# Scores of two groups in one visit of TensorE, one bank for both FFNs' sums, projections moved in a macaron block on one Trainium2 core

## The reference

```python
x = x + 0.5 * ffn(layernorm(x), w_gate_up, w_proj)
x = x + attention(layernorm(x), Wq, Wk, Wv, Wo)
x = x + 0.5 * ffn(layernorm(x), w_gate_up, w_proj)

def ffn(x, w_gate_up, w_proj):             # hidden width 2048
    gate, up = split(x @ ternary(w_gate_up).T)   # ternary: per 64 weights round(w / mean|w|) * mean|w|, bf16
    return rms_norm(silu(gate) * up) @ ternary(w_proj).T

def attention(x, Wq, Wk, Wv, Wo):          # 32 heads of 16, blocks of 128 tokens
    # each token attends to itself and the 128 tokens before it: its own block of keys and the one before
    return softmax(mask(q k^T / 4)) @ v @ Wo.T
```

## Time and profile before

| | before |
|---|---|
| median of 3 runs | 2028.27 us |
| the profiled execution | 2030.56 us, span 2028.7 us |
| TensorE busy | 1919.7 us, 95% |
| VectorE, ScalarE, GpSimd busy | 1541.2, 1493.1, 510.9 us |
| mean granted TensorE clock | 0.98 |
| share of the transfers' queue | 75.9% |

### The profile page before, as it was taken

The page is one execution under the profiler, slowest core; times in us unless marked ns, Lnnn a source line. Parts: engine busy times, 40 slices in busy tenths (PEclk is TensorE's granted clock), DMA queues, the critical chain, the costliest instruction groups (busy, mean ns, idle before and its releaser), DMA issues. The chain is left out here.

```text
span 2028.7 us, 37471 instructions
## 1 busy us (share of the span) xinstructions
PE 1919.7 (95%) x12447; PEld 898.9 (44%) x12688; DVE 1541.2 (76%) x4079; ACT 1493.1 (74%) x2871; POOL 510.9 (25%) x559
## 2 busy tenths in 40 slices
PE   6678899999999999999999999999999999999887
PEld 3353344444444444444444444444444444444332
DVE  8966788777876888777777888777786788777673
ACT  6837777777776777777776777777776777768672
POOL 2012222232223222322222223222223232221100
PEclk8889999999999999999999999999999999999898
DMA  7336888788887878777896788878886788768772
GB/s 233 121 71 112 147 153 147 132 141 159 149 156 126 156 145 153 136 145 150 154 159 125 138 155 153 149 131 154 159 155 120 141 153 165 144 120 154 131 136 52
DMA packets 1031648, 287.81 MB, mean 142 GB/s; under 512 B 1016096, under 2 KB 1017120, under 8 KB 1030944
## 3 DMA queue, kind: packets, MB, share of 16 engines
q1 hardware_dynamic: 1031456, 285.41, 75.9%
HBM read 25.17 MB, written 8.39 MB: 17 GB/s over the span
## 5 line engine op out<-in xcount | busy, mean ns | idle before, releaser
L731 ACT ACTIVATE masked<-masked,exp_bias,exp_scale 128x256 f32<-128x256 f32 (+1 forms) x1024 | 503.8, 562 | 8.6
L1095 PE MATMUL ps_yy<-wp_t,ht 128*128 128x512 bf16 x1978 | 481.0, 383 | 14.4 <-DMA ht<-hh 11.7
L1049 PE MATMUL ps_gu<-wgu_t,xt_A 128*128 128x512 bf16 x1940 | 473.8, 382 | 11.2 <-DVE hid L859 2.5
L1049 PE MATMUL ps_gu<-wgu_t,xt_C 128*128 128x512 bf16 x1958 | 472.6, 379 | 5.3 <-DMA xt_C<-xh 0.5
L605 ACT ACTIVATE hh<-hid 128x512 f16<-128x512 f32 x256 | 161.0, 629 | 276.3 <-DVE hid L865 271.0
L876 DVE CUSTOM_DVE_ANT_0 masked<-ps_s,mask 128x256 f32<-128x256 f32 (+1 forms) x1024 | 337.4, 385 | 0.7 <-PE ps_s L1085 0.6
L865 DVE SCALAR_TENSOR_TENSOR hid<-ps_gu,h_scale_u,hid 128x512 f32<-128x512 f32 x252 | 188.9, 750 | 185.0 <-PE ps_gu L1049 184.7
L1095 PEld LDWEIGHTS ps_yy<-wp_t,ht 128*128 128x128 f16 x2016 | 197.9, 99 | 254.5 <-DMA ht<-hh 13.5
L1049 PEld LDWEIGHTS ps_gu<-wgu_t,xt_A 128*128 128x128 f16 x2048 | 198.6, 98 | 243.3 <-issue 6.3
L1049 PEld LDWEIGHTS ps_gu<-wgu_t,xt_C 128*128 128x128 f16 x2048 | 193.4, 98 | 222.5 <-issue 2.4
L850 DVE TENSOR_TENSOR prob<-masked,prob 128x1024 f16<-128x1024 f32 (+1 forms) x256 | 278.9, 1089 | 2.4 <-ACT prob L743 2.4
(11 more groups left out here) (148 smaller groups left out, 1892.8 us busy)
## 6 DMA issues: line engine op xcount, KB each, us to landing
stream<-in_L_attn_x_dram SPq DMA_DIRECT2D x32, 256.0 KB, 3.3
pt<-prob SPq DMA_TRANSPOSE x512, 3.2
out_dram<-stream SPq DMA_DIRECT2D x32, 256.0 KB, 2.4
prob<-in_L_ffn_w_gate_up_dram SPq DMA_DIRECT2D x4, 1024.0 KB, 5.6
ht<-hh SPq DMA_TRANSPOSE x256, 3.3
stream<-in_L_ffn_w_gate_up_dram SPq DMA_DIRECT2D x3, 1024.0 KB, 5.6
stream<-in_L_ffn_w_proj_dram SPq DMA_DIRECT2D x2, 1024.0 KB, 4.9
prob<-in_L_ffn_w_proj_dram SPq DMA_DIRECT2D x2, 1024.0 KB, 4.8
```

The lines of the kernel that those rows point to most:

```text
L731: t = act.activation(p, p, ACT.Exp, bias=exp_bias[:, 4 * g + h:4 * g + h + 1], scale=exp_scale[:, 0:1])
L1049: t = pe.matmul(bank[:, :], xt[s][:, part, k, :], wgu_t[:, k, at:at + CH], start=(k == 0 and part == 0), stop=(k == KD - 1 and part == 1))
L1095: t = pe.matmul(ps_y[s][:, :], ht[:, n % HRING, i, :], wp_t[:, 4 * c + i % 4, :], start=(c == 0 and i == 0), stop=(c == NC - 1 and i == 2 ...
```

## The change

- The scores of an even and the odd group after it are issued together in the even step, right behind the gate matmuls; the odd group's go to `ps_x` (the bank that was C's sum) and `ps_m`. VectorE takes the maxima of both in the even step.
- A and C share the bank `ps_y`; the first `down` of a unit sequence waits until the sum before was added.
- PV goes between down and up. The projections are at the steps 8, 10, 12 and 22, all even, and use the bank `ps_u` in steps without a unit, `ps_m` otherwise, where they now wait for the maxima (`bank_free`).
- ScalarE makes the normalised tokens' high part (xh) behind the exps, and the high part of the probabilities ahead of the hidden quarter's. VectorE's low part of the probabilities stands behind the hidden product, at the end of its own step.
- K's transpose is issued in two parts, the first for the pairs of heads 0 to 3. The transposes of the probabilities stand one step earlier in SyncE's program, ahead of ht.

```diff
-    LN_B, XHAT_B, SPLIT_B = 5, 6, 7
-    Q_AT, K_AT, V_AT = 8, 9, 11
+    LN_B, XHAT_B, SPLIT_B = 6, 6, 7
+    Q_AT, K_AT, V_AT = 8, 10, 12
-    PROB = SCORES + 1
-    NORM = PV + 1
-    SPLIT_O, WO_AT = NORM + 7, 23
+    NORM = PV
+    SPLIT_O, WO_AT = NORM + 7, 22
-        ps_y = {"A": ps_yy[:, 0:CH], "C": ps_yy[:, CH:2 * CH]}
+        ps_y, ps_x = ps_yy[:, 0:CH], ps_yy[:, CH:2 * CH]
+        ps_sc = ((ps_s[:, 0:CH], ps_s[:, CH:2 * CH]), (ps_x, ps_m))
...
+        def projected(step):
+            return ps_m if ffn_at(step)[0] else ps_u
...
-                    transpose(kt[:, :, b % BPS, :], k4[:, :, :, :].rearrange("p a b c -> p (a b c)"), t_k)
+                    for part, pairs in enumerate((slice(0, 4), slice(4, HEADS // 2))):
+                        transpose(kt[:, pairs, b % BPS, :],
+                                  k4[:, 2 * pairs.start:2 * pairs.stop, :, :].rearrange("p a b c -> p (a b c)"),
+                                  t_k[part])
...
@@ VectorE, step_of
                 b, g = group_at(step, SCORES)
-                if b is not None:
-                    masked_max(b, g)
+                if b is not None and g % 2 == 0:
+                    masked_max(b, g)
+                    masked_max(b, g + 1)
...
+                b, g = group_at(step, SCORES)
+                if b is not None:
+                    prob_lo(b, g)
...
@@ TensorE, step_of
+            def bank_free(step):
+                if projected(step) is ps_m:
+                    need(pe, d_mx, 2 * groups_by(step + 1, SCORES))
+                else:
+                    s, b, c = ffn_before(step)
+                    if s:
+                        pe.wait_ge(d_h[s], 4 * b + c + 1 + (NC if s == "A" else 0))
...
+                b, g = group_at(step, SCORES)
+                if b is not None and g % 2 == 0:
+                    if step == SCORES:
+                        pe.wait_ge(a_lo, 8)
+                    need(pe, d_mx, 2 * (8 * b + g))
+                    projections_taken(step - 2)
+                    if g == 0:
+                        pe.wait_ge(t_q, 16 * (b + 1))
+                        pe.wait_ge(t_k[0], 16 * (b + 1))
+                    if g == 2:
+                        pe.wait_ge(t_k[1], 16 * (b + 1))
+                    scores(b, g, ps_sc[0])
+                    scores(b, g + 1, ps_sc[1])
```

More of the change, by code:

```diff
@@ L298, in macaron @@
         assert len(AT_STEP) == len(GATES) == 2 * NB * NC - NC
+        assert all(QUARTERS[n][1:3] == QUARTERS[n - n % NC][1:3] for n in range(len(QUARTERS)))
         def gate_at(step):
@@ L453, in _ @@
                 load_x(b)
-            for step in range(FIRST_STEP, STEPS + 1):
+            for step in range(FIRST_STEP, STEPS + 2):
                 b = block_at(step, Q_AT + 1)
@@ L694, in step_of @@
                         act.wait_ge(g_fill, 3)
[L695 to L700, removed]
+                    copy(v[:, b % BPS, :, 0:DK], head_view(projected(step - 1)[:, :]), p_v, b + 1, a_v, 2.0 ** -V_LOG2)
                 if step == LAST_SPLIT:
@@ L733, in step_of @@
                     t.then_inc(a_exp, 1)
-                s, bf, c = ffn_at(step)
-                if s:
-                    hidden_hi(s, bf, c, place(step), 4 * bf + c + 1 + (NC if s == "A" else 0))
+                for s, offset in SPLITS:
+                    b = block_at(step, offset)
+                    if b is not None and in_steps(s, b) and not (s == "B" and b == 0):
+                        split_free(act, step, s)
+                        copy(xh[:, 0, :], xhat[:, :], g_xh[s], b + 1, a_xh[s])
+                b = block_at(step, SPLIT_O)
+                if b is not None:
+                    output_hi(b)
                 b, g = group_at(step, SCORES)
@@ new lines, in step_of @@
+                if step == LAST_WO:
+                    add_output(LAST, ps_m)
+                    norm_stats("C", LAST, d_x2, NB)
+                s, bf, c, n = gate_at(step)
+                if s:
+                    gated(s, bf, c, n)
+                b = block_at(step, LN_B)
+                if b is not None and b > 0:
+                    norm_stats("B", b, d_x1, b + 1)
+                b = block_at(step, LN_C)
+                if b is not None and b < LAST:
+                    norm_stats("C", b, d_x2, b + 1)
@@ L947, in step_of @@
+                b = block_at(step, LN_A)
+                if b is not None and in_steps("A", b):
+                    norm_stats("A", b, x_in[b % 2], 16 * (b // 2 + 1))
                 b, g = group_at(step, NORM)
@@ L993, in step_of @@
                         attention_weight(n)
-                b = block_at(step, WO_AT + 1)
-                if b is not None and b < LAST:
-                    add_output(b)
+                b = complete("A", step, 2)
+                if b is not None:
+                    add_ffn("A", b, d_x1)
+                b = complete("C", step, 2)
+                if b is not None:
+                    add_ffn("C", b, d_x3)
                 s, bf, c = ffn_at(step)
@@ L1069, in attention_weight, with project, scores @@
                 t.then_inc(a_tr, 1)
-            def project(m, tokens, done):
+            def project(m, tokens, done, bank):
                 for k in range(KD):
                     for n, (part, w) in enumerate(((0, wat_hi), (0, wat_lo), (1, wat_hi))):
-                        t = pe.matmul(ps_m[:, :], tokens[:, part, k, :], w[m][:, k, :], start=(k == 0 and n == 0),
+                        t = pe.matmul(bank[:, :], tokens[:, part, k, :], w[m][:, k, :], start=(k == 0 and n == 0),
                                       stop=(k == KD - 1 and n == 2))
                 t.then_inc(done, 1)
-            def scores(b, g):
+            def scores(b, g, banks):
                 at_block = b % BPS
@@ L1083, in scores @@
                         rows = slice(64 * o, 64 * o + 3 * DK)
-                        at = o * CH + pair * 2 * P
-                        t = pe.matmul(ps_s[:, at + P * first_half(b):at + 2 * P],
+                        t = pe.matmul(banks[o][:, pair * 2 * P + P * first_half(b):(pair + 1) * 2 * P],
                                       qt[rows, b % QRING, 2 * g + pair, :],
@@ L1175, in output_projection, with projections_taken @@
                 need(pe, d_x2, b)
-                project(O, ot, p_wo)
+                project(O, ot, p_wo, bank)
+            def projections_taken(step):
+                for offset, done in ((Q_AT, d_q), (K_AT, d_k), (V_AT, d_v), (WO_AT, d_x2)):
+                    b = block_at(step, offset)
+                    if b is not None:
+                        pe.wait_ge(done, b + 1)
             def step_of(step):
                 if step == LAST_WO:
-                    output_projection(LAST)
+                    need(pe, d_mx, 2 * 8 * NB)
+                    output_projection(LAST, ps_m)
                 s, b, c, n = gate_at(step)
```

168 lines of the change are left out of this document (72 added, 96 removed).

## The result

After: 2031.91 us, median of 9 runs (2029.52 to 2037.31). Before, on the same chip: 2027.07 us, median of 9 runs (2025.95 to 2029.26). The ratio over all these executions is 1.0028 (it is not that of the two medians), 95% interval 1.0016 to 1.0039: 0.3% slower, where 2010 us had been forecast. The profiled execution of the changed kernel took 2029.5 us and is among its quickest; the one of before is among its slower ones, so their spans stand 1.1 us apart the other way. The traces tell where the time is, the medians how much.

What follows compares the result with a forecast made beforehand. TensorE was taken to bound the 1657 us middle, latency the 220 us around it. Profiled 2030.6 - 22.6 (pairs) + 4.2 (projection's wait) = 2012.2; the median lies 2.3 below the profiled run, so 2010 us, range 2003 to 2015.

Steps and rivals of the forecast that it cites:

- What bounds the kernel: TensorE bounds the 1657 us middle, where nothing in its step waits; latency bounds 220 us around it.
- Scores in pairs: TensorE goes into the scores half as often in the middle, saving 0.20 us a pair: 113 pairs, -22.6 us.
- Rival A: At the paired scores each group pays the drain: eight matmuls 0.66 us, a pair saves 0.09, time 2022; chance 0.10.
- Wait 1: In even steps the projection waits for VectorE's eight maxima; 0.2 us charged in 21 of 28 blocks, +4.2 us.
- Rival B: VectorE's eighth maximum comes late in even steps and stalls TensorE's projection: slower, put at 2042 us; chance 0.11.
- Normalised tokens' high part behind the exps: ScalarE's copy comes some 3 us later; POOL waits for it, its result is used a step later: hidden.
- All stay hidden, by my count: Reordered transfers on the one queue all land before TensorE wants them; smallest slack 0.3 us, for K's first quarter.
- Rival D: A new block's scores wait for K's first quarter: 0.5 us in 28 blocks, 14 us, time 2024; chance 0.05.
- The ends: Start and end of the kernel, with Q's bank wait of 4.1 us each to be had: set to 0, bounds -8 and +12.
- Rival C: In steps without units a pair pays one group of maxima openly, 11 us in all: 2018 to 2022; chance 0.14.

Runs made afterwards that it cites:

- e1: The changed kernel with ScalarE's high-part copies of A's, B's and C's normalised tokens back ahead of tanh and exps; 2033.69 us, ratio 1.0025 to the kernel before.
- e9: The changed kernel with the first part of K's transpose one place earlier in SyncE's program, ahead of ht; 2039.71 us, ratio 1.0059 to the kernel before.
- e13: The changed kernel with only C's high-part copy of the normalised tokens back ahead of the exps; 2014.23 us, ratio 0.9927 to the kernel before.
- e6: The changed kernel with A's and C's high-part copies ahead of the exps, B's still behind them; 2011.07 us, ratio 0.9908 to the kernel before.
- e12: e6 without pairs: each group's scores and maxima in its own step, all in the scores' bank; 2068.55 us, ratio 1.0196 to the kernel before.
- e2: The changed kernel with K's transpose in one piece again; 2118.67 us, ratio 1.0447 to the kernel before.
- e3: The changed kernel without pairs where one of a pair's two steps has no FFN unit; 2053.4 us, ratio 1.0122 to the kernel before.
- e10: e6 with the down projection as TensorE's last work of a step at both ends; 2011.73 us, ratio 0.9925 to the kernel before.
- e11: e6 with the down projection as TensorE's last work of a step at the end alone; 2010.83 us, ratio 0.9914 to the kernel before.

## Why the prediction was wrong

*What bounds the kernel:* right. The middle is TensorE's pitch, and every wait put there shows in the time: the changed kernel, e1 and e9 have 10.8, 17.6 and 17.9 us of waits there, e13 has 1.9, and their middles are 9.8, 18.0 and 18.6 us longer than e13's.

*Scores in pairs, 0.20 each:* right. Eight matmuls take 0.54 (0.55 forecast), with 128 keys 0.33; four pairs make a block of 57.60 us instead of 58.45, so 0.21 a pair (e6, e13, and e12 the other way). Rival A, 0.66, is out: the fixed part is paid once for two groups behind each other. The Trainium skill (TensorEngine Tiling (Array Packing), Key Properties) says that a change of the tiling mode drains TensorE and a change of tile alone does not. The trace agrees with it as far as the 0.54 us go.

*Wait 1, +4.2:* not needed. The changed kernel has no such wait between the landmarks. The chain is as tight as counted, though: one copy of 0.6 us ahead of it (B's, in e1) makes 19 waits of 0.9. Rival B's place was right, and it does not fire in this kernel.

*The step that failed* is the treatment of the moved copy: "Normalised tokens' high part behind the exps: ... the copy was waited for by POOL, whose result is used a step later. Hidden." POOL's result is used by the multiplications a step later, but its first user is a transpose in SyncE's program, and that one stands ahead of the transposes of the probabilities, ht and K. I followed the copy's data and not the queue behind its reader. With it falls "All stay hidden, by my count": K's first quarter was given 0.3 us of slack from the time its data is ready, as if the queue were free then; it is issued 3.0 us later (996.82 to 999.86). A second error hid a part of this one. The landing was put at up to 4.3 us, the time of the whole transpose, and the first quarter takes at most 2.64. Counted from the odd step's start (994.71), the prediction had K's quarter landed by 7.0 and wanted at 7.3; it was issued at 5.15 and wanted at 7.47 (1002.50 less the wait of 0.32). With the whole transpose's landing time every block would have waited some 2 us, as e2 did.

Rival D named this wait and its size came out (0.5 us in 28 blocks, 14 us, 2024; measured 15.0 us in 24 waits over the run), by luck, since no row gave its 0.5, and it had 0.05 of the chance: I weighed only how long the landing would take. What D's sum lacked is the ends: between the changed kernel and e13 the start differs by 3.3 us (1.4 of it ahead of any copy of C) and the end by 4.9 besides the 9.8 of the middle, 18.0 together in the profiles; the medians 2031.91 and 2014.23 say 17.7, the ratios 1.0028 and 0.9927 some 20.

*The ends, 0:* right for all the rest of the change taken together, by e13, whose start and end are those of before within 0.3 us, in one execution of each. The 4.1 us that were "to be had" at each end were misread in part: the 12 matmuls of Q that take 4.29 us instead of 2.60 stand in a stretch with a granted clock of 0.62 (222.2 to 226.6 us of the kernel before), so 1.7 of the 4.1 are the clock's and not the bank's. Rival C is not borne out as far as it was tried (e3, e12).

With C's copy undone the time falls into the forecast's range. e13's profiled execution took 2011.7 us, where the sum said 2012.2, but that this close is luck: it sets a quick execution of e13 against a slow one of before. By the ratio e13 is at 0.9927, where 2010 of 2028.27 us is 0.9910, so it wins 15 us of the 18 that were forecast. The terms did not come out singly either. Its 26 blocks are 18.8 us shorter than before, the pairs alone would give 22.1, and the difference of 3.3 is not the wait that was charged with 4.2: short waits for ht, xt_B and K show 1.9 of it, and the rest shows in no wait. e6, e10, e11 and e13 beat both kernels (2011.07, 2011.73, 2010.83 and 2014.23 us); which of the four is best, their runs cannot tell.

## What to carry to other kernels

When an instruction is moved later, follow not only its result to the user that computes with it, but to the first queue that it passes through, and ask what is issued in program order behind it: here 0.6 us of ScalarE's work, moved by one place, cost some 18 us, most of it through four transfers behind one that was late. A slack is counted from the moment the queue is free, not from when the data is ready. And a change of several parts that comes out at nothing can hold a good part and a bad one; undoing them one at a time, down to a single copy, gave 0.7 to 0.9% that the whole did not show.

## What the runs showed that I had not expected

- Splitting K's transpose is worth 87 us here (2118.67 against 2031.91): the first quarter lands at most 2.64 us after its issue (999.86 to 1002.50, with a wait for it at the end), the whole one takes 4.3 and is issued no sooner. 60 us of it are waits; in the middle the rest goes with a granted clock of 0.98 instead of 1.00.
- Waits do not vanish in a full program, they change names: mending K's wait by order (e9) gave 16.5 us to ht, mending it with all copies (e1) gave 17.4 to the maxima. Only the kernels that made the head of the queue ready earlier without making the maxima late (e6, e13) gained time.
- Taking the pairs out costs 57 us, though each spares 0.21: 22 of it are theirs in the middle, the other 35 waits, a lower clock and longer ends that no step of the prediction would have found. The ends grow by 24.5 us, at most some 15 of it by the clock; what makes TensorE wait there stays open.
